# A two-layer attention kernel: self-attention's head halves turned and added, low weight halves in short pieces on GpSimd, roots ahead of biases

## The reference

```python
x = x + _L0_xattn_ref(_layernorm(x), ctx_768, ...)
x = x + _L0_attn_ref(_layernorm(x), ...)
x = x + _L0_ffn_ref(_layernorm(x), ...)

def _L0_attn_ref(tokens, norm_w, Wq, Wkv, Wout, q_gamma, k_gamma):
    H, QH, DH, SOFTCLAMP = 8, 16, 64, 50.0
    x = _rmsnorm(tokens, norm_w)
    q, (k, v) = heads(x @ Wq), heads(x @ Wkv)       # 16 query heads, 8 key and value heads
    q, k = _mh_rmsnorm(q, q_gamma), _mh_rmsnorm(k, k_gamma)
    sim = tanh(einsum('bhgid,bhjd->bhgij', q, k) / SOFTCLAMP) * SOFTCLAMP * DH ** -0.5
    attn = softmax(where(causal, -max, sim))
    out = einsum('bhgij,bhjd->bhid', attn, v)       # sums over g: two query heads share a value head
    return out @ Wout
```

## Time and profile before

| what | us |
|---|---|
| median of 3 runs (lowest, highest) | 1830.26 (1827.12, 1839.62) |
| the profiled execution | 1831.6 |
| its span | 1829.8 |
| TensorE busy, share | 1775.2, 97% |
| DVE busy, share | 1348.4, 74% |
| ACT busy, share | 1017.9, 56% |
| GpSimd busy, share | 939.3, 51% |
| self-attention, from its first projection of tile 0's keys to the last turn of the loop | 655.2 to about 771.6 |
| feed-forward, to its last matmul | 768.7 to 820.6 |

### The profile page before, as it was taken

How to read it: one execution, slowest core, us unless ns; L and a number is a source line. 1 busy time by engine, 2 the same in 40 slices (tenths; PEclk the granted TensorE clock), 3 DMA queues, 4 the chain that set the end, 5 groups by cost and what they waited for, 6 DMA issues and landing times.

```text
span 1829.8 us, 44764 instructions
## 1 busy us (share of the span) xinstructions
PE 1775.2 (97%) x17870; PEld 1548.1 (85%) x17870; DVE 1348.4 (74%) x2790; ACT 1017.9 (56%) x2138; POOL 939.3 (51%) x1178
## 2 busy tenths in 40 slices
PE   7999999999999999999999999999999999999998
PEld 6888888888878778899999999999999986668887
DVE  6888888888888877667766767676776755767775
ACT  5677676767667745455444445444444434526664
POOL 3787777777787527446433334333433313514553
PEclk9999999999999999999999999999999999989999
DMA  5121111211110110044222222222223007051111
GB/s 166 39 73 39 38 39 38 63 49 38 38 38 3 60 51 1 22 121 121 64 64 64 64 64 64 64 64 64 86 72 90 7 5 299 1 187 32 33 32 16
DMA packets 50750, 113.11 MB, mean 62 GB/s; under 512 B 4928, under 2 KB 37264, under 8 KB 49008
## 3 DMA queue, kind: packets, MB, share of 16 engines
q1 hardware_dynamic: 46128, 105.13, 19.2%
q0 software_dynamic: 4416, 5.12, 1.6%
HBM read 105.78 MB, written 5.37 MB: 61 GB/s over the span
## 4 chain that ended last, share of the span: by engine, by line
PE 78%; DVE 13%; ACT 4%; issue 3%; DMA 1%; POOL 1%; SPq 0%; DVEq 0%; POOLq 0%; ACTq 0%
PE ps L104 8%; PE ps L166 7%; PE ps L1782 6%; PE ps L514 5%; PE ps L495 5%; PE ps L472 4%; DVE arenaR L1903 3%; DVE arena L1909 3%; PE ps L2774 3%; PE ps L1783 3%; PE ps L489 3%; PE ps L424 2%; PE ps L1706 2%; PE ps L2748 2%; PE ps L2749 2%
## 5 line engine op out<-in xcount | busy, mean ns | idle before, releaser
L617 DVE TENSOR_REDUCE arena<-ps 128x1 f32<-128x400 f32 (+1 forms) x512 | 257.7, 565 | 84.1 <-PE ps L472 83.7
L777 ACT ACTIVATE arena<-ps 128x384 f32<-128x384 f32 (+1 forms) x512 | 223.3, 524 | 94.9 <-PE ps L495 93.8
L1782 PE MATMUL ps<-arenaR 128*128 128x386 f32 x768 | 266.3, 392 | 0.0
L878 POOL TENSOR_TENSOR arena<-arena 128x512 f32<-128x512 f32 (+1 forms) x152 | 197.4, 1299 | 77.4 <-ACT arena L777 69.1
L2013 ACT CAST arenaR<-ps 128x512 fp32r<-128x512 f32 (+1 forms) x256 | 123.0, 507 | 183.4 <-PE ps L166 174.5
L1783 PE MATMUL ps<-arenaR 128*128 128x194 f32 x768 | 194.8, 254 | 0.0
L166 PE MATMUL ps<-ident,wsb 128*128 128x128 f32 (+1 forms) x832 | 160.0, 273 | 2.2 <-ACT wsb L2038 1.7
L2038 ACT ACTIVATE wsb<-ps,arena 128x1200 f32<-128x1200 f32 x64 | 80.9, 1264 | 131.9 <-DVE arena L1962 131.9
L1783 PEld LDWEIGHTS ps<-arenaR 128*128 128x128 f32 x768 | 146.8, 191 | 0.0
L1782 PEld LDWEIGHTS ps<-arenaR 128*128 128x128 f32 x768 | 145.4, 189 | 0.7 <-DVE arenaR L1903 0.5
L1903 DVE TENSOR_TENSOR arenaR<-ps,arenaR 128x512 fp32r<-128x512 f32 (+1 forms) x256 | 138.2, 582 | 3.9 <-ACT arenaR L2013 3.5
(11 more groups left out here) (387 smaller groups left out, 5112.0 us busy)
## 6 DMA issues: line engine op xcount, KB each, us to landing
wsb<-in_ctx SPq DMA_DIRECT2D x16, 1152.0 KB
wsb<-in_ctxT SPq DMA_DIRECT2D x16, 800.5 KB, 4.9
wsb<-in_ctxT SPq DMA_DIRECT2D x32, 400.2 KB, 7.3
gu<-in_m_gu SPq DMA_DIRECT2D x8, 1536.0 KB, 19.1
arena<-in_ctxT SPq DMA_DIRECT2D x15, 800.5 KB, 5.1
arena<-in_ctxT SPq DMA_DIRECT2D x30, 400.2 KB, 7.4
dn<-in_m_dn SPq DMA_DIRECT2D x8, 768.0 KB, 10.0
wsb<-in_f_w SPq DMA_DIRECT2D x2, 1024.0 KB, 5.9
```

Source lines behind the costliest of these rows:

```text
L617: e.tensor_reduce(mx4[n % 2][:, u, i:i + 1], ps[:, at("look", n, i, u), 0:400 + (i == 3)], AX.X, ALU.max).then_inc(c.maxed.at((n, i, u)), 1)
L777: e.activation(v[:, u, 0:128 * GN[s]], ps[:, at("st", n, s, u), 0:128 * GN[s]], ACT.Exp).then_inc(c.exp_a.at((x0, n, s, u)), 1)
L878: e.tensor_tensor(sums_p[0:k], sums_p[0:k], v[0:k, :, 128 * t:128 * t + 128], ALU.add).then_inc(added_p.at((n, s)), 1)
L1782: e.matmul(o, PTh[:, t, :], v[:, t, 0:386], start=(t == 0), stop=False)
```

## The change

1. **Turned halves.** `fold` becomes `turn_o`: 8 transposes of 128x128 into two banks (3 and 4), with each head still apart. ACT copies the first halves of the heads to `oT` (`take_half`), and DVE then adds the second halves from PSUM (`add_half`). `finish` on TensorE waits for that sum (`added`). `output` goes through the heads in an order that leaves bank 4 to the fifth pair, since that bank is still being read.
2. **Order of the loop.** `scores(t)` stands ahead of `finish(t-2)` on TensorE. DVE's `finish` stands between the two masks, its `moments` are put off to a later turn (`weigh(t-3)`), and `norm_tile` of tiles 0 to 5 is spread over turns 5 to 9; tiles 6 and 7 follow the loop.
3. **Start of the loop.** Tile 7's query bank is projected in two parts, the last behind `scores(0)`, and its banks begin at 3; tile 6's and tile 7's squares are summed later (tile 7's in two halves, in turns 2 and 3), so that `norms(1)` covers tiles 4 and 5 alone and GpSimd takes the roots of tiles 6 and 7 (`root_of`).
4. **GpSimd's queue.** The low half of `w1` is made in four subtractions of 512 columns ahead of `root_of(7)`; then come `normalise(7)`, all eight `root_pool`, the low half of `w2` in four pieces, and the biases of tiles 0 to 6.
5. **End of the first attention.** For its last head group the sums of part 2 are made by TensorE (`summed_by_pe`): three terms more, 12 matmuls or 24 records, in place of three additions of 512 columns on DVE.
6. **Feed-forward.** Its banks are turned by one (bank 4 is in use), and ACT takes its high half before it loads the table for gelu.

```diff
-        def fold(t):
+        def turn_o(t):
             w.wait_ge(*c.o_norm((sa, t, 1)))
             w.wait_ge(*emptied[3])
-            w.wait_ge(*c.in_const("small"))
             for b in range(2):
                 for k in range(4):
-                    p = e.matmul(ps[:, 3, 128 * k + 64 * b:128 * k + 64 * b + 64], flat(o1[:, 8 * b + 2 * k:8 * b + 2 * k + 2, :]),
-                                 c.fold, start=True, stop=True)
+                    p = c.turn(e, ps[:, 3 + b, 128 * k:128 * k + 128], flat(o1[:, 8 * b + 2 * k:8 * b + 2 * k + 2, :]))
             p.then_inc(c.o_turned.at((sa, t)), 1)
-            emptied[3] = c.a_out((sa, t))
+            emptied[3] = emptied[4] = added(t)
...
+        def add_half(t):
+            w.wait_ge(*first_half(t))
+            e.tensor_tensor(both_halves(oT), turned_half(1), both_halves(oT), ALU.add).then_inc(added.at(t), 1)
...
         for t in range(1, NT + 2):
             then.dve(e, w, t)
             if t < NT:
                 take_q(t)
+            if t == 1:
+                project_q0()
+            if t >= 3:
+                weigh(t - 3)
+            if t == NT:
+                then.dve_last(e, w)
             if t <= NT:
                 output(t - 1)
+            if t < NT:
+                mask(t, 0)
             if t >= 2:
                 finish(t - 2)
             if t < NT:
-                mask(t)
-            if t == 1:
-                squares(NT - 1)
-            if t == NT:
-                then.dve_last(e, w)
+                mask(t, 1)
+            if t <= NT:
+                add_half(t - 1)
+            if t in (2, 3):
+                squares_last(t - 2)
+        weigh(NT - 1)
...
         for t in range(NT):
             if t == NT - 1:
-                root_of_last()
+                then.pool_split(e, w, "w1")
+            if t >= NT - 2:
+                root_of(t)
             normalise(t)
...
-        for tile in {6: (0, 1), 7: (2, 3), 8: (4, 5), 9: (6,)}.get(t, ()):
+        for tile in {5: (0,), 6: (1, 2), 7: (3,), 8: (4,), 9: (5,)}.get(t, ()):
             norm_tile(c, e, w, into, tile)
...
     def pool_ahead(e, w):
-        for k, v, hi, lo in (("w1", m.fw1, w1h, w1l), ("w2", m.fw2, w2h, w2l)):
-            w.wait_ge(*w_hi(k))
-            e.tensor_tensor(lo, v, hi, ALU.subtract).then_inc(w_lo.at(k), 1)
         for t in range(NT):
             root_pool(c, e, w, into, t)
-            if t:
-                add_bias(e, w, t - 1)
+        pool_split(e, w, "w2")
+        for t in range(NT - 1):
+            add_bias(e, w, t)
```

## The result

| what | before | after |
|---|---|---|
| median (lowest, highest), 20 runs each | 1830.64 (1826.60, 1840.11) | 1827.11 (1822.90, 1831.08) |
| the profiled execution, its span | 1831.6, 1829.8 | 1822.9, 1821.1 |
| TensorE's records | 17870 | 17830 |

The ratio of the times is 0.9977, with a 95% interval of [0.9967, 0.9987]: 4.2 us less, between 2.4 and 6.0; the medians differ by 3.5. The forecast was 1826.0 in a range from 1817 to 1834.

A forecast was written before the change was run, and what follows sets the result against it. The prediction took TensorE's queue alone to bound the loop, without gaps at 8.42 us a turn. Its terms summed to -8.65 us, with one low-clock spell of 3.0 us -5.7, so 1831.6 became about 1826, range 1817 to 1834.

The forecast's parts named there:

- end of the first attention: End of the first attention: TensorE's wait for DVE and DVE's additions go, 24 records come, -0.95 us.
- clock at the loop's start: Loop's start: the clock stays at the higher level, so `fold`, turns and part of the scores speed up, -3.0 us, uncertain.
- turned halves: Each loop turn: 8 transposes replace `fold`'s 2.10 us, gaining 1.13 us a tile, times 8, -9.0 us.
- scores ahead of `finish`: Loop order on TensorE: 4.3 us from scores to the next output covers the 3.3 needed, nothing lost, 0.
- stall and its low spell: Head of turn 5: DVE waits for GpSimd's roots, TensorE's scores wait, +4.1 us; one low-clock spell, +3.0 us.
- pieces of `w1`: Turn 2: GpSimd's `w1` pieces meet masks that have 1 us in hand, 0.
- pieces of `w2`, start of feed-forward: Start of feed-forward: four GpSimd pieces hold back DVE's low halves of gelu, between 0 and 2.8 us, taken as +1.0.
- Rival 1: Turn 5: the root is in time, so the stall and its low spell go, 1819 us; 10%.
- Rival 2: Loop's start: GpSimd's power holds DVE for its length, delaying tile 0's second mask, +3.5 us, 1829.4 us; 8%.
- Rival 3: Turns 1 to 4: DVE becomes the bound while GpSimd works without pause, four turns cost 6.4 us, 1832 us; 10%.
- Rival 4: Whole loop: transposes don't hold the clock, a turn costs 6.1 us more, seven turns 43, 1866 us; 6%.
- rival 5: Loop: two low-clock spells, at the start and behind the stall, 1829 us, 14%; or none at all, 1823 us, 17%.

The follow-up runs named there:

- e9: e1 with the sums of the first attention's last head group added by DVE again instead of TensorE: 1823.53 us, one run.
- e10: e8 with `fold`'s 8 matmuls back in place of the 8 transposes and no addition of halves on DVE: 1823.70 us, ratio 0.9963 to before.
- e8: e7 with DVE's norm tiles behind the copy of the queries, tile 6's moments and norm tile moved into the loop: 1816.33 us, ratio 0.9914 to before.
- e1: The changed kernel with `norm_tile` of tile 0 moved from turn 5 to turn 6: 1821.24 us, ratio 0.9941 to before.
- e7: e1 with `w1` pieces waiting for tile 2's second mask and `w2` pieces behind the roots of tiles 2 and 3: 1817.41 us, ratio 0.9927 to before.
- e5: e1 with the low half of `w1` again made in one GpSimd subtraction of 2048 columns: 1823.31 us, one run.
- e6: e1 with the last part of tile 7's query bank projected ahead of tile 0's scores again: 1825.38 us, one run.
- e4: e1 with `w1` pieces moved behind the roots of tiles 2 and 3, `w2` pieces behind those of tiles 4 and 5: 1818.09 us, ratio 0.9925 to before.

## Why the prediction was right, point by point

**The time.** 1827.1 against 1826.0. The sum for the touched places was -5.7 us and -5.4 was measured. That it came so near is partly luck, since some terms were wrong, and cancelled; and the range, 1817 to 1834, holds the old median too. What the forecast had earned is the stall, named ahead with its place, its chain and its length.

| term | forecast | measured | from |
|---|---|---|---|
| end of the first attention | -0.95 | -1.38 | table; e9 |
| idle time at the loop's start | -1.0 | -1.55 | to output 0 |
| clock at the loop's start | -3.0 | -3.2 | scores, `fold`, turns of the earlier trace rows against the earlier trace rows |
| turned halves | -9.0 | -5.4 | e10 to e8, in the new order |
| scores ahead of `finish` | 0 | about -3 | before to e10 |
| half taken ahead, end of the loop | -0.5 | -0.8 | to up, before to e10 |
| small new waits | +0.7 | in the -5.4 | e8's turns 2 to 4, 0.1 to 0.2 each |
| stall and its low spell | +4.1, +3.0 | +5.9 | after to e1 |
| pieces of `w1` | 0 | +1.4 | e1 to e7, turns 2 and 3 |
| pieces of `w2`, start of feed-forward | +1.0 | +2.6 | to down; 1.6 are the pieces (e7) |
| sum | -5.7 | -5.4 | |

Three small terms are left out and cancel: a wait of 0.25 us that goes at the start, 0.3 in turn 7 between e1 and e7, and against them the 0.53 that only e8 has.

**Turned halves: the term that was furthest off.** The forecast took the whole of `fold`'s 2.10 us as what the transposes replace, and 0 for the order. 0.27 of the 2.10 were TensorE's wait for ACT's tanh, which the order takes away and the transposes don't. So "the loop is TensorE's queue and nothing else" was misread; and where the forecast asked what the new order costs the output, it didn't ask what the old one cost the turns. e10 shows 1.73 for `fold` in the new order and 7.94 for the turn. The gain of a gap-free turn is 1.35 (8.42 to 7.07), more than the 1.13 forecast, and 0.48 of it is the order's. For seven turns the order's part is about 3 us: e10's turns add up to 53.74, before's to 60.21, less 3.2 for the low spell and 0.25 for a wait 56.8. Of these 3, 0.3 are turn 3 before (8.71 us), whose output waited for the long mask of the earlier trace rows; there DVE's mask didn't come in time either. And "it fits", said of DVE's 6.3 us of work a turn, was true of the sum only. In e1 the turns 2, 3, 4 and 6 have 0.33, 1.37, 0.23 and 0.48 over 7.07, so that there the exchange is worth 3.8 and not 5.4.

**The stall** was right in place, mechanism and size: DVE idle for 4.93 us (4.6 or more), TensorE for 4.75 (4.1). The chain was read with a root begun at the end of turn 3, and it did begin there, at 723.73. What was mis-sized is the low spell: 1.6 us, and not the 3.0 of the earlier trace rows. In windows of 1 us the clock is down from 733 to 741, about as long as before (705 to 712), but for three of these microseconds TensorE has nothing to do anyway.

**Pieces.** "The masks have 1 us in hand: 0" failed. TensorE's hand was there, but two masks are held, not one. DVE's masks of turn 2 in after, and the pieces beside them:

```profile
711.39 1.79 DVE L1258 TENSOR_TENSOR sat<-sat,sa 128x512 f32<-128x512 f32 x1 [0.88 <-ACT sat L1378]
...
713.45 1.45 DVE L1258 TENSOR_TENSOR sat<-sat,sa 128x512 f32<-128x512 f32 x1
```

```profile
710.10 5.95 POOL L1614 TENSOR_TENSOR ffw<-wsb,ffw 128x512 fp32r<-128x512 f32 x4
```

1.1 and 0.76 us together are over the 1 us. The output behind them takes 2.43 instead of 2.00 us, and DVE's queue carries the rest into `take_q(3)`, for which `scores(3)` waits 0.88. A piece is 1.5 us there, not 1.26. In feed-forward the four of `w2` cost 1.6. The bound of 2.8 held, and the value chosen was low.

The remaining 1.0 (25.40 to 26.40 in e7) isn't the norm tile that e8 moves. The traces name a candidate that the forecast left out: part 4 also puts GpSimd's biases behind one another, and in e7 all eight run beside DVE's first low halves of gelu. The first of these, before and in e7, with GpSimd's biases in e7 and TensorE's wait there:

```profile
777.61 0.68 DVE L1515 TENSOR_TENSOR ffa<-ffg,ffa 128x512 fp32r<-128x512 f32 x1
```

```profile
763.16 1.22 DVE L1568 TENSOR_TENSOR ffa<-ffg,ffa 128x512 fp32r<-128x512 f32 x1
```

```profile
762.35 6.99 POOL L1629 TENSOR_TENSOR x<-x,biasb 128x256 f32<-128x256 f32 x8
```

```profile
768.91 11.41 PE L104 MATMUL ps<-xB,ffw 128*128 128x512 f32 x46 [0.63 <-DVE xB L1550]
```

ACT's gelu behind it starts 0.6 us later after the first up matmul than before, and TensorE waits 0.63. No run moves the biases, so this is not shown.

**Rivals.** Rival 1 fell with the stall. Rival 2 fell by a row: the power of tile 7's root runs from 724.09 to 728.27, and a mask inside it has its usual length:

```profile
727.37 0.69 DVE L1258 TENSOR_TENSOR sat<-sat,sa 128x512 f32<-128x512 f32 x1 [0.56 <-ACT sat L1378]
```

The Trainium skill (SBUF — State Buffer, section "SBUF: two separate sides") has an exclusive lock for the whole instruction. GpSimd's subtractions behave like that here (e5: 3.81 us for a mask). The power doesn't, and there the measurement decides. Rival 3 was wrong as a bound on every turn, but its mechanism is the +1.4 of turns 2 and 3. Rival 4 fell: with 20 transposes a turn, e8's window over the whole loop has a clock of 1.00:

```profile
700.00:780.00 80.00, 78.08 (x795) 67.06 (x794) 61.63 (x114) 49.36 (x81) 49.02 (x80) 1.00 0.22 67
```

The Trainium skill (TensorE: Matmul & The Clock Gate, section "Part 4: PE-mode transpose") says that transposes don't engage the full clock. This window doesn't bear that out for transposes among matmuls. Of rival 5's cases neither came: in after's loop there was one spell, behind the stall, as forecast.

**Other signs.** `turn_o` takes 0.87 (0.97 forecast) and the turn 7.07 (7.3). The output of tile 0 comes without a wait (under 0.5 us late), with one of 0.24 behind it. A piece takes 1.25 us alone (1.3). The end of the first attention gains 1.38. After, DVE waits 0.64 us for GpSimd there, TensorE 0.25 for DVE:

```profile
649.38 0.32 DVE L665 TENSOR_SCALAR arena<-arena,small 128x64 f32<-128x64 f32 x1 [0.64 <-POOL arena L898]
```

```profile
654.48 1.13 PE L104 MATMUL ps<-arena 128*128 128x256 f32 x4 [0.25 <-DVE arena L669]
```

## What to carry to other kernels

When the bottleneck's turn gets shorter, walk the queues of the engines that serve it again with the new length: 5.9 of the 11 us that this change could bring went into one helper that stood one turn too early, and a row of numbers brought them back. Where an operation of one engine ends only behind the other's, as the masks did beside GpSimd's subtractions, the longest single instruction costs, not the sum; cut it, and let the pieces start when the other has just gone by. And before a start-to-start time is taken as the price of an instruction, look at what the next one waits for: `fold`'s 2.10 us held 0.27 of waiting for ACT that no bracket showed, and the release of a PSUM bank was its cause.

## What the hardware showed that was not expected

- **Eight f32 matmuls of 64 columns have 1.83 us from start to start behind the scores (before, turn 7) and 1.73 behind `finish` (e10).** The scores are 64x64 matmuls, `finish` and `fold` 128x128 ones. In e10 the first weight load of `fold` starts at 727.22, 0.21 us ahead of its matmul; before, at 734.36, with the matmul. That this load was hidden in e10 would explain the 0.10; it was only argued.
- **The clock fell behind idle time of TensorE, but not behind all of it.** It was down in the loop behind a wait of 4.75 us (after), one of 2.05 (e5), waits of 0.79, 0.46 and 0.25 (before) and waits of 0.79, 0.94 and 0.88 with smaller ones between (e6). With the wait of 4.75 gone (e1), the clock stayed up. It also stayed at 1.00 with one of 0.88 and smaller ones (e1), with one of 1.20 and one of 0.89 two turns apart (e4), and with one of 1.68 ahead of the loop (e9). Which pattern decides is open. The price of one spell was 1.6 to 3.2 us.
- **GpSimd's power of 24 columns leaves a mask of DVE alone for its 4.18 us; a subtraction of 2048 columns holds it to its end.** Both read and write SBUF only.
